# A cross-attention kernel: values of two steps in one run, and what stands around it

## What is computed

```python
q = _split_heads(hidden_states @ Wq.T, H)          # (2, 20, 2048, 32)
k = _split_heads(text @ Wk.T, H)                   # (2, 20, 77, 32)
v = _split_heads(text @ Wv.T, H)
scores = jnp.einsum('bhsd,bhld->bhsl', q, k) * sm_scale
probs = jax.nn.softmax(scores, axis=-1)
out_text = _merge_heads(jnp.einsum('bhsl,bhld->bhsd', probs, v))
return out_text @ Wo.T + bo + residual
```

## Time and profile before

| | us |
|---|---|
| three runs | 423.13, 423.15, 428.57 (median 423.15) |
| the profiled execution, its own time | 422.98 |
| its span in the trace | 421.2 |
| PE busy | 414.0 (98%) |
| ACT, POOL, DVE busy | 301.1, 299.9, 271.4 |

### The profile page before, as it was taken

How to read it: one execution, slowest core, us unless ns; L and a number is a source line. 1 busy time by engine, 2 the same in 40 slices (tenths; PEclk the granted TensorE clock), 3 DMA queues, 4 the chain that set the end, 5 groups by cost and what they waited for, 6 DMA issues and landing times.

```text
span 421.2 us, 8311 instructions
## 1 busy us (share of the span) xinstructions
PE 414.0 (98%) x2567; PEld 232.4 (55%) x2567; DVE 271.4 (64%) x552; ACT 301.1 (71%) x585; POOL 299.9 (71%) x262
## 2 busy tenths in 40 slices
PE   8999999999999999999999999999999999999997
PEld 6877775677776644444444444444444444444443
DVE  0354676766678789976578666756577655655733
ACT  1738888857678887888668875888668875967720
POOL 8327799999679696777659594678659594674560
PEclk9999999999999999999999999999999999999999
DMA  8998635554966456334753347335753347345203
GB/s 281 369 315 276 233 113 210 170 181 159 292 217 207 158 183 226 128 125 166 238 200 126 128 149 254 125 127 179 242 182 128 130 148 248 126 164 193 98 25 126
DMA packets 41925, 77.33 MB, mean 184 GB/s; under 512 B 5280, under 2 KB 6688, under 8 KB 41888
## 3 DMA queue, kind: packets, MB, share of 16 engines
q1 hardware_dynamic: 30944, 57.21, 39.2%
q10 hardware_dynamic: 10944, 19.67, 14.5%
HBM read 33.40 MB, written 10.49 MB: 104 GB/s over the span
## 4 chain that ended last, share of the span: by engine, by line
PE 85%; DVE 5%; issue 2%; DMA 2%; SPq 2%; ACT 2%; POOL 1%; DVEq 0%; ACTq 0%
PE ps_q L955 28%; PE ps_o L955 26%; PE ps_s L1022 9%; PE ps_pv L1029 7%; PE ps_m L1006 5%; PE ps_den L1034 4%; PE ps_o L926 2%; PE ps_m L1081 2%; DMA x_f<-in_x 2%; DVE tops L795 1%; DVE wq L791 1%; SPq L375 1%; POOL x_lo L448 1%; PE ps_q L1081 1%; PE ps_o L1081 1%
## 5 line engine op out<-in xcount | busy, mean ns | idle before, releaser
L457 POOL TENSOR_TENSOR p_lo<-p_f,p_hi 77x512 f16<-77x512 f32 x160 | 182.6, 1161 | 89.8 <-ACT p_hi L596 88.8
L592 ACT ACTIVATE p_f<-ps_s 77x512 f32<-77x512 f32 x160 | 94.5, 591 | 29.9 <-PE ps_s L1022 29.6
L955 PE MATMUL ps_o<-attn,wo 128*128 128x512 f16 x435 | 109.0, 381 | 0.9 <-DVE sums L816 0.6
L734 DVE TENSOR_REDUCE mx<-ps_m 128x4 fp32r<-128x308 f32 x160 | 69.3, 475 | 53.1 <-PE ps_m L1006 52.0
L596 ACT ACTIVATE p_hi<-ps_s 77x512 f16<-77x512 f32 x160 | 93.6, 585 | 2.4 <-PE ps_den L1034 2.3
L955 PE MATMUL ps_q<-x,wq 128*128 128x512 f16 x375 | 85.2, 379 | 0.0
L1022 PE MATMUL ps_s<-q_packed,k_packed 128*77 128x512 f32 x160 | 66.8, 460 | 0.2
L955 PEld LDWEIGHTS ps_o<-attn,wo 128*128 128x128 f16 x435 | 35.5, 98 | 52.2 <-issue 17.8
L955 PEld LDWEIGHTS ps_q<-x,wq 128*128 128x128 f16 x375 | 35.3, 98 | 43.5 <-issue 3.5
L1006 PE MATMUL ps_m<-k_diag,q_hi 128*128 128x308 f32 x160 | 43.3, 350 | 0.4 <-ACT q_hi L577 0.4
L723 DVE SCALAR_TENSOR_TENSOR q_lo<-ps_q,q_scale,q_hi 128x512 fp32r<-128x512 f32 x25 | 18.7, 750 | 34.0 <-ACT q_hi L575 33.6
(11 more groups left out here) (126 smaller groups left out, 596.6 us busy)
## 6 DMA issues: line engine op xcount, KB each, us to landing
q_packed<-q_hi SPq DMA_DIRECT2D x80, 256.0 KB, 2.5
x_f<-in_x SPq DMA_DIRECT2D x45, 256.0 KB, 4.6
q_packed<-q_lo SPq DMA_DIRECT2D x40, 256.0 KB, 3.3
x_res<-in_x ACTq DMA_DIRECT2D x35, 256.0 KB, 2.7
out<-x_res ACTq DMA_DIRECT2D x35, 256.0 KB, 2.8
wq_sb<-in_wq SPq DMA_DIRECT2D x10, 320.0 KB, 4.4
wo_sb<-in_wo SPq DMA_DIRECT2D x10, 320.0 KB, 3.9
wk_sb<-in_wk SPq DMA_DIRECT2D x8, 320.0 KB, 5.3
```

Source lines behind the costliest of these rows:

```text
L457: nc.gpsimd.tensor_tensor(p_lo[:, i, :], p_f[:, i, :], p_hi[:, i, :], ALU.subtract).then_inc(plo_done, 1)
L592: nc.scalar.activation(p_f[:, i, :], ps_s[i % 2][0:L, :], ACT.Exp, scale=SCALE).then_inc(pf_done, 1)
L734: nc.vector.tensor_reduce(mx[:, g % RS, :, tt], ps_m[tt % 2][:, 0:HG * L].rearrange("p (h k) -> p h k", k=L), AX_X, ALU.max).then_inc(max_ ...
L955: last = nc.tensor.matmul(ps[:, :], w[:, k, P * c:P * (c + 1)], a[:, c, :], start=(c == 0 and n == 0), stop=(c == G - 1 and n == 2))
```

## The change

**Values.** From step 7 on, steps with odd n ("odd steps", `is_pair`) run the values of steps n-2 and n-1 in one run of 40 matmuls; even steps run none. Steps 1 to 5 and the one behind step 39 run one step's values as before. The first half goes to `ps_o`, the second to `ps_pv`, and the sums of both to `ps_den`: the weights `half_ones` are ones in 16 of 32 columns and zeros in the others, so each half fills 16 rows of each quarter. One `invert_den` (a transpose and a reciprocal of twice the elements) serves both; `spread_den`, the transpose back, and `normalise` run once for each.

**Buffers.** `p_hi` and `p_lo` have two sets. `p_f` has three places (`PF`) for single heads in place of four. `q_lo` has two places in place of three. `sum_tops` writes into `ps_den`, and no longer waits for an output tile; the next burst waits for `sums_read`, and `sum_tops` for `den_done`.

**Order.** Since the first half takes `ps_o`, the output tile of an odd step runs whole at the step's end, behind `normalise` of the first half. Query projections move to the step's front and middle in all steps. ACT, DVE and POOL have other orders in odd steps. `attn_split_at` makes the halves of the attention of tiles 1, 3, 5 in two steps, four chunks in (t+1, 0) and the fifth in (t+1, 1). In the last steps other banks are used. The hardware loop is gone (`run`).

```diff
+    def is_pair(n):
+
+        return n > G + 1 and n % 2 == 1 and n < NU
+
+    def values_at(n):
+
+        if is_pair(n):
+            return (n - 2, n - 1)
+        return (n - 1,) if 1 <= n <= G or n == NU else ()
+
...
-        if isinstance(t, int) and (t, g) == (NB - 1, G - 1):
+        if (t, g) == (NB - 1, G - 1):
             return NB - 1, (0, 1, 2)
-        if isinstance(t, int) and t == NB:
+        if t == NB:
             return NB - 1, (3, 4) if g == 0 else ()
-        return (t - 1, range(G)) if g == 0 and exists(t - 1) else (t, ())
+        if g == 0 and exists(t - 1):
+            return t - 1, range(G - 1) if (t - 1) % 2 else range(G)
+        if g == 1 and exists(t - 1) and (t - 1) % 2:
+            return t - 1, (G - 1,)
+        return t, ()
...
+                if n >= 2:
+                    pool.wait_ge(pv_done, bursts_with(n - 2))
+                nc.gpsimd.tensor_tensor(p_lo[:, n % 2, i, :], p_f[:, (HG * n + i) % PF, :], p_hi[:, n % 2, i, :],
...
+                if HG * n + i >= PF:
+                    act.wait_ge(plo_done, HG * n + i + 1 - PF)
+                nc.scalar.activation(p_f[:, (HG * n + i) % PF, :], ps_s[i % 2][0:L, :], ACT.Exp,
                                      scale=SCALE).then_inc(pf_done, 1)
-                if exists(shift(t, g, -1)[0]):
-                    act.wait_ge(pv_done, nth(t, g))
-                nc.scalar.activation(p_hi[:, i, :], ps_s[i % 2][0:L, :], ACT.Exp,
+                if n >= 2:
+                    act.wait_ge(pv_done, bursts_with(n - 2))
+                nc.scalar.activation(p_hi[:, n % 2, i, :], ps_s[i % 2][0:L, :], ACT.Exp,
...
+                pair = is_pair(nth(t, g))
+                if xt is not None and pair:
+                    x_high(xt, range(0, 3))
+                if exists(t) and not (xt is not None and pair):
                     exponentials(t, g, 2)
                 for v in value_group(t, g) if exists(t) else ():
                     v_high(v)
@@ -651,28 +677,38 @@
                     copy_max(*shift(t, g, 1))
                 for v in value_group(t, g) if not exists(t) else ():
                     v_high(v)
+                if exists(t) and xt is not None and pair:
+                    exponentials(t, g, 2)
+                early_attn = pair and tuple(chunks) == (G - 1,)
+                if early_attn:
+                    attn_high(at, chunks)
                 if exists(t):
                     exponentials(t, g, 3)
-                attn_high(at, [c for c in ((0, 1, 2, 3) if first_split else (2, 3)) if c in chunks])
+                behind_queries = pair and len(chunks) == G
+                if not early_attn and not behind_queries:
+                    attn_high(at, chunks)
                 for tile in out_tiles(*shift(t, g, 1)):
                     load_residual(*tile)
-                attn_high(at, [c for c in (4,) if c in chunks])
                 wq_half_high(wq_half_high_at(t, g))
                 w_half_high(wo_half_high_at(t, g), wo_sb, wo_16, wo_up, wo_up_done, wo_scaled, wo_hi16)
-                if x_scaled_at(t, g) is not None:
+                if x_scaled_at(t, g) is not None and not pair:
                     x_scale(x_scaled_at(t, g))
-                if xt is not None:
+                if xt is not None and not pair:
                     x_high(xt, range(0, 4))
                 if exists(shift(t, g, 2)[0]):
                     q_high(*shift(t, g, 2))
                 if xt is not None:
-                    x_high(xt, (4,))
+                    x_high(xt, (3, 4) if pair else (4,))
+                if x_scaled_at(t, g) is not None and pair:
+                    x_scale(x_scaled_at(t, g))
+                if behind_queries:
+                    attn_high(at, chunks)
...
+            def invert_den(n):
+
+                burst = bursts_so_far(n)
+                dve.wait_ge(pv_done, burst)
                 nc.vector.transpose(rden[:, :], ps_den[:, :]).then_inc(den_done, 1)
-                dve.wait_ge(den_done, nth(t, g) + 1)
-                nc.vector.reciprocal(rden_t[:, :], rden[:, 0:TB:D]).then_inc(inv_done, 1)
-                dve.wait_ge(inv_done, nth(t, g) + 1)
-                nc.vector.transpose(rden[:, :], rden_t[:, :].unsqueeze(2).to_broadcast([P, TB // D, D])
+                dve.wait_ge(den_done, burst)
+                nc.vector.reciprocal(rden_t[:, :, :], rden[:, :].rearrange("p (j h r) -> p h j r", h=2, r=D // 2)[:, :, :, 0]
+                                     ).then_inc(inv_done, 1)
+
+            def spread_den(n, at):
+
+                half = values_at(at).index(n)
+                dve.wait_ge(inv_done, bursts_so_far(at))
+                if half == 1:
+                    dve.wait_ge(norm_done, n)
+                nc.vector.transpose(rden[:, :], rden_t[:, half, :].unsqueeze(2).to_broadcast([P, TB // D, D])
                                     ).then_inc(rden_done, 1)
 
-            def normalise(t, g):
+            def normalise(n, at):
...
+            def pair_step(t, g):
+                n = nth(t, g)
                 at, chunks = attn_split_at(t, g)
-                last_t, last_g = shift(t, g, -1)
+                has_next_max = exists(shift(t, g, 1)[0])
+                invert_den(n)
+                spread_den(n - 2, n)
+                if has_next_max:
+                    reduce_max(*shift(t, g, 1), 0)
+                    reduce_max(*shift(t, g, 1), 1)
+                normalise(n - 2, n)
+                if has_next_max:
+                    reduce_max(*shift(t, g, 1), 2)
+                    reduce_max(*shift(t, g, 1), 3)
+                if exists(shift(t, g, 3)[0]) and x_in_half(shift(t, g, 3)[0]):
+                    set_q_scale(*shift(t, g, 3))
                 if has_sums(t, g):
                     read_sums(t, g)
+                    set_scales(t, g)
+                spread_den(n - 1, n)
+                normalise(n - 1, n)
+                for c in ENDS_DVE:
+                    if at_an_end(at) and c in chunks:
+                        attn_low(at, c)
+                if exists(shift(t, g, 2)[0]):
+                    q_low(*shift(t, g, 2))
+                find_tops(t, g)
+                wq_half_low(wq_half_high_at(t, g))
+                for tile in out_tiles(t, g):
+                    finish_out(*tile)
...
-                    pe.wait_ge(outs_done, nth(*out_tiles(t, g)[0]))
+                    pe.wait_ge(sums_read, sums_up_to(n - 1))
+                pe.wait_ge(den_done, bursts_so_far(n))
...
+                both = values_at(n)
+                if both[0] >= 1:
+                    pe.wait_ge(norm_done, both[0])
+                if sums_up_to(n - 1):
+                    pe.wait_ge(sums_read, sums_up_to(n - 1))
+                if is_pair(n):
+                    done = [tile for tile in out_tiles(*divmod(n - 1, G)) if out_bank(*tile) is ps_o]
+                    pe.wait_ge(outs_done, nth(*done[-1]) + 1)
+                if n == 1 or n == G + 2:
+                    pe.wait_ge(const_done, 6)
+                for h, m in enumerate(both):
+                    t, g = divmod(m, G)
+                    b, hi, lo = t // BPB, p_hi[:, m % 2, :, :], p_lo[:, m % 2, :, :]
+                    bank = ps_o if is_pair(n) and h == 0 else ps_pv
+                    weights = half_ones[:, h, :] if is_pair(n) else ones[:, :]
+                    pe.wait_ge(phi_done, HG * (m + 1))
+                    attend(bank, v_hi, b, hi, g, start=True, stop=False)
+                    attend(bank, v_lo, b, hi, g, start=False, stop=False)
+                    add_up(weights, hi, start=(h == 0), stop=False)
+                    pe.wait_ge(plo_done, HG * (m + 1))
+                    attend(bank, v_hi, b, lo, g, start=False, stop=True)
+                    last = add_up(weights, lo, start=False, stop=(m == both[-1]))
+                last.then_inc(pv_done, 1)
...
+                n, query = nth(t, g), shift(t, g, 2)
+                pair, has_query, has_max = is_pair(n), exists(query[0]), exists(max_t)
+                first = () if pair and has_query else tiles[0:1]
+                if values_at(n):
+                    values(n)
+
+                def queries(*chunks):
+                    if has_query:
+                        project_q(*query, chunks)
+
+                def output(*chunks):
+                    for tile in first:
+                        project_out(*tile, chunks)
+
+                if n == NU:
+                    for chunks in ((1,), (2,), (3, 4)):
+                        last_tiles(chunks)
+                    return
+                queries(0)
+                scores(t, g, 0, batch(t))
+                scores(t, g, 1, batch(t))
+                if has_max:
+                    max_scores(max_t, max_g, 0, batch(max_t))
+                    max_scores(max_t, max_g, 1, batch(max_t))
+                queries(1, 2)
+                if not has_query:
+                    output(0, 1)
+                if has_max:
+                    max_scores(max_t, max_g, 2, batch(max_t))
```

(20 more changed lines are left out.)

194 lines of the change are left out of this document (84 added, 110 removed).

## The result

Four executions of the changed kernel took 446.52, 447.03, 449.24 and 452.57 us (median 448.13), those of the kernel before 423.13 to 428.57 (median 423.32). The ratio is 1.057, 95% interval 1.046 to 1.069: slower by 25 us, where the prediction had 7.7 us and a range up to 437. The profiled execution is the one of 446.52; its span is 444.7 us, 23.5 more than before.

A forecast was written before the change was run, and what follows sets the result against it. PE was taken as the bound, with a matmul under way for 414.0 of 421.2 us. Savings of 3.7 and 3.8 against added waits gave +7.7 on 422.98, plus 0.2 for the median: 430.9 us, range 419.5 to 437.

The forecast's parts named there:

- Bursts joined: Steps 6 to 40: 18 bursts of values instead of 35, each costing 0.22 us beyond its matmuls; 3.7 us less.
- The sums: Steps with the small matmul of sums: the wait for sums_read goes, the matmul stays; 3.8 us less, bounds 2.4 and 5.2.
- Step 6: Front of step 6, now without a burst: queries wait for DVE's q_lo of query 7; 3.1 us more.
- The plain odd step holds: Plain odd steps: q_lo done at 9.9, before the step's end at 10.36; maxima and unrolling the loop costed at nothing.
- Steps 12, 22, 32: Third score there waits for exponentials, since five x_scale follow q_hi the step before; 2.7 us more, 0.9 each.
- Steps 15 to 17, 25 to 27 and 7, 17, 27: Late q_lo behind attn_hi and POOL's lows, 2.5 us more; behind three x_high, 1.0 us more.
- Steps 9 to 16: Steps making weights in halves: ACT's and DVE's pieces make q_lo and maxima late; 4.0 us more, bounds 1.7 and 5.4.
- The end: Step 39: attn_hi follow the fourth exponentials, so the last tiles wait for DVE's low half; 1.9 us more.
- The clock: Rival: PE's clock falls to 1.2 GHz behind step 6's new gap, 4 us more, 434.9 us; chance 0.05.

The follow-up runs named there:

- e1: Changed kernel, but in odd steps DVE makes the query weights' low half ahead of q_lo and the searches for largest magnitudes; 441.17 us, ratio 1.042.
- e3: Changed kernel, but in step 39 DVE makes all three low halves of the last attention, POOL only its four p_lo; single execution, 449.94 us.
- e4: Changed kernel, but step 39 makes chunk 0's high half behind the second head's exponentials, its low half behind the first normalise; 443.31 us, ratio 1.045.
- e2: Changed kernel with matmuls that nobody reads put into the four long gaps, ahead of steps 6, 14, 16 and the last tiles; 440.41 to 448.78 us, ratio 1.044.
- b3: Kernel before, but in step 5 DVE's low half of chunk 0 waits for three high halves instead of one; 428.49 us.

## Why the prediction was wrong

Its range ended at 437; the time was 448.

- **Bursts joined, 3.7 less: right.** 0.21 for a pair of plain steps, the 0.22 of the prediction.
- **The sums, 3.8 less: mis-sized,** 2.85 measured, within the bounds. The step that failed is reading step 6's 0.93 as sums.
- **Step 6, 3.1 more: right** (3.07), for its reason.
- **The plain odd step holds: right.** No wait in steps 19 to 21, 23 to 26 and 29 to 31 of over 0.25, and no cost of the unrolled loop there.
- **Steps 12, 22, 32, 2.7: right in place,** 2.0 in size. **Steps 15 to 17, 25 to 27 and 7, 17, 27, 3.5 together:** 2.85 in steps 17, 18, 27 and 28.
- **Steps 9 to 16, 4.0: failed,** 9.2 and two falls of the clock. "In step 13 `q_hi` starts at 8.5 + 0.7 + 1.5 = 10.7 and `q_lo` ends at 12.2: 1.7 late" was right to 0.1 (`e1` left 1.63). The step took `q_lo` for the last thing that the moved queries need. They read the weights' halves too, made one step before at the end of DVE's order. The change had put them there, behind `q_lo` and searches of 1.5 and 1.9 us (steps 13 and 15); with the low half ahead of `q_lo` again (`e1`), 3.97 became 1.63 and 2.98 became 0.64. The wait for `wq_lo16` stood in `project_q`, and the prediction followed only the wait that was quoted beside it.
- **The end, 1.9: mis-sized,** 4.58. ACT came as reckoned; DVE's low half was costed at its 1.39 of before, but half of that was waiting for POOL (it takes 0.68 with POOL idle, `e3`), and it grew to 3.49 behind more of POOL's work (`e3`, `e4`).
- **The clock: the rival that came true,** given one chance in twenty, for step 6 alone and with 4 us. It cost 1.7 there, but it came four times: 6.2 us, and it went with the waits (`e1`, `e4`) or with idle matmuls in them (`e2`). The row that spoke for it was missed: 1.00 in every window before was no evidence about gaps of 3 us, since the longest idle stretch in those windows was 0.4.

Of the 15.8 us between the sum on the profiled execution, 430.7, and 446.5, the clock is 6.2, steps 9 to 16 5.2, the end 2.7, the sums 1.0; the small terms, the wait of step 36 and the 1.6 of short waits make up the rest. The waits that the prediction listed, it listed at the right places; what it lacked was the second consumer of a late engine and the price of a long gap.

## What to carry to other kernels

When an operation is moved ahead, list every semaphore it waits for, and for each the whole queue of its maker, not only the wait that held it before. Sum gaps by place: here those from 2.36 us on were paid again in clock and those up to 1.63 weren't, so that cutting a gap of 3.97 to 1.63 made its two steps 3.5 us shorter (24.67 to 21.18). And read a duration as suspect when the same instruction has different ones: DVE's low half of one chunk took 0.7 us with POOL idle and 1.3, 3.5, 5.1 and 6.2 beside it.

## What the runs showed of the hardware

A DVE instruction with two SBUF operands that started while POOL worked waited for one POOL instruction or for several in a row: it ended behind one `p_lo` after 1.25 us, behind POOL's four low halves after 6.16 and 5.13, behind the last three of five `x_lo` after 4.20, and 0.55 to 0.69 behind the POOL instruction each time. Where POOL had another one ready, DVE still got in ahead of it in `b3` and in the short case of step 5, and that one took some 0.5 longer. In step 5 both cases came up with the same instructions. That this is what makes the kernel before fall on two values 5 us apart is inferred: `b3` makes the longer value at will, and kernels without the instruction on DVE don't show it.

The clock fell behind every gap of 2.36 us and more past step 5, and behind none of up to 1.63; matmuls that nobody reads, put into three such gaps (`e2`), kept it up there. The length of the low clock behind a gap wasn't fixed: 3.4 and 6.1 us behind 3.07, 2.8, 5.2 and 5.9 behind 3.96.
